# A fused convolution block's output stage: leaky step moved into ScalarE's activation, residual add shared out anew

## The reference

```
x = x + L0(_gn(x), ...)      # two gelu layers
x = x + L1(_gn(x), kernel)   # 4x4 filter
x = x + L2(_gn(x), ...)      # window attention without softmax
x = x + L3(_gn(x), ...)      # 3x3 involution, batch norm, leaky ReLU
```

```
mean = jnp.mean(yout, axis=(0, 1, 2))
var = jnp.var(yout, axis=(0, 1, 2))
yn = (yout - mean) * jax.lax.rsqrt(var + BN_EPS) * gamma + beta
return jnp.where(yn >= 0, yn, LEAKY_ALPHA * yn)
```

## Time and profile before

| | |
|---|---|
| median of 3 runs | 1075.73 us |
| lowest and highest | 1072.3 and 1078.36 us |
| the profiled execution's own time | 1075.53 us |
| its span in the profile | 1072.9 us |
| busy TensorE (matmul) | 783.7 us, 73% of the span |
| busy VectorE | 701.1 us, 65% |
| busy ScalarE | 560.3 us, 52% |
| busy GpSimd | 325.0 us, 30% |

### The profile page before, as it was taken

The page is one execution under the profiler, slowest core; times in us unless marked ns, Lnnn a source line. Parts: engine busy times, 40 slices in busy tenths (PEclk is TensorE's granted clock), DMA queues, the critical chain, the costliest instruction groups (busy, mean ns, idle before and its releaser), DMA issues. The chain is left out here.

```text
span 1072.9 us, 28694 instructions
## 1 busy us (share of the span) xinstructions
PE 783.7 (73%) x12508; PEld 564.6 (53%) x12508; DVE 701.1 (65%) x1085; ACT 560.3 (52%) x581; POOL 325.0 (30%) x265
## 2 busy tenths in 40 slices
PE   5589986897998547844888759979975487346664
PEld 4344442897887437511334319969854384024443
DVE  6556665997555993592223359965459925979993
ACT  4899992342444206357899913424442072525553
POOL 1111111740003880060000026200048700636665
PEclk8899997898999767855799969989986587557776
DMA  9322220000000000000000000000000000003556
GB/s 300 113 64 68 61 71 2 1 2 2 4 4 4 1 1 20 2 0 1 2 2 2 2 1 1 2 2 4 4 4 1 1 20 1 0 1 118 156 157 196
DMA packets 59932, 37.54 MB, mean 35 GB/s; under 512 B 1952, under 2 KB 59424, under 8 KB 59808
## 3 DMA queue, kind: packets, MB, share of 16 engines
q1 hardware_dynamic: 59808, 35.71, 11.0%
HBM read 18.93 MB, written 16.78 MB: 33 GB/s over the span
## 5 line engine op out<-in xcount | busy, mean ns | idle before, releaser
L376 PE MATMUL ps<-work,w2d 32*32 32x512 f32 x2048 | 155.1, 649 | 22.5 <-ACT work L636 15.7
L624 ACT ACTIVATE work<-X,l0s 128x2048 f32<-128x2048 f32 x64 | 133.5, 2089 | 5.1 <-SPq L320 3.8
L363 PE MATMUL ps<-work,cst 32*32 32x512 f32 x2048 | 100.8, 654 | 40.5 <-ACT work L636 21.6
L636 ACT ACTIVATE work<-ps 128x2048 f32<-128x2048 f32 x64 | 119.9, 1873 | 19.3 <-PE ps L363 19.3
L773 DVE SCALAR_TENSOR_TENSOR X<-ps,X 128x1024 f32<-128x1024 f32 x32 | 39.2, 1225 | 136.0 <-PE ps L376 136.0
L1099 POOL TENSOR_TENSOR work<-cst,work 128x512 f32<-128x512 f32 x64 | 69.6, 1109 | 178.7 <-SPq L320 158.0
L376 PEld LDWEIGHTS ps<-work,w2d 32*32 32x32 f32 x2048 | 63.1, 110 | 88.5 <-issue 75.4
L653 ACT ACTIVATE work<-ps 128x512 f32<-128x512 f32 x80 | 47.8, 597 | 110.6 <-PE ps L430 110.6
L441 PE MATMUL ps<-cst,work 128*128 128x143 f32 x640 | 95.2, 294 | 0.2 <-DVE X L823 0.2
L870 DVE TENSOR_TENSOR work<-ps,cst 128x512 f32<-128x512 f32 x64 | 44.3, 692 | 70.7 <-PE ps L477 70.7
L276 PE MATMUL ps<-ST,work 32*128 32x512 f32 x256 | 58.6, 1007 | 43.6 <-DVE work L1005 18.7
(11 more groups left out here) (105 smaller groups left out, 1557.2 us busy)
## 6 DMA issues: line engine op xcount, KB each, us to landing
out<-work SPq DMA_DIRECT2D x64, 256.0 KB, 3.2
work<-x SPq DMA_DIRECT2D x16, 512.0 KB, 5.2
work<-x SPq DMA_DIRECT2D x32, 256.0 KB, 2.9
work<-choose SPq DMA_DIRECT2D x8, 128.0 KB, 2.7
cst<-consts SPq DMA_DIRECT2D x1, 1009.5 KB, 9.5
cst<-consts SPq DMA_DIRECT2D x1, 64.0 KB, 1.9
```

Of the source, the lines that this page charges most:

```text
L363: last = pe.matmul(ps[C * k4:C * k4 + C, g, :], wg[rows, m, C * g:C * g + C], yb[rows, m % 2, k4 * BANK:(k4 + 1) * BANK], start=True, stop ...
L376: last = pe.matmul(ps[C * g:C * g + C, 4 + b, :], diag[rows, m, :], zb[rows, k % ZDEEP, g, :], start=(m == 0), stop=(m == MULTI - 1))
L624: act.activation(yb[:, k % 2, :], X[:, s * PIX + i * CHUNK:s * PIX + (i + 1) * CHUNK], ACT.Gelu, scale=l0s[:, at:at + 1], bias=l0s[:, at + ...
L636: act.activation(zb[:, (s * UNITS + k) % ZDEEP, :, :], ps[:, 0:4, :], ACT.Gelu).then_inc(s_zs, 1)
```

## The change

The activation that applies the batch normalisation's scale and bias uses Prelu with alpha 0.3 instead of Identity, and does the leaky step with it; `leaky` on VectorE is gone. GpSimd now waits for the activation (`s_fy`) instead of for VectorE, and adds the residual to blocks 0 and 1 in one instruction of 128x1024 and to block 2 in one of 128x512. VectorE adds it to block 3 in one scalar_tensor_tensor of 128x512 (`add_last`, (y x 1.0) + x), in the place in its order where `leaky` stood, and raises a semaphore of its own, `s_fd`, for which TensorE waits before it transposes block 3.

```diff
--- before.py
+++ after.py
@@ -119,9 +119,9 @@
 
             return X5[:, ds(s * 4, 4), ds(w, 1), :].rearrange("p b o h -> p (b o) h")
 
-        def group_columns(s, j, b):
-
-            return X[:, s * PIX:(s + 1) * PIX].rearrange("p (b n) -> p b n", b=4)[:, b:b + 2, TILES * j * H:TILES * (j + 1) * H]
+        def group_columns(s, j, b, n):
+
+            return X[:, s * PIX:(s + 1) * PIX].rearrange("p (b n) -> p b n", b=4)[:, b:b + n, TILES * j * H:TILES * (j + 1) * H]
 
         def rows4(v):
             return v.rearrange("p (b h) -> p b h", b=4)
@@ -245,8 +245,8 @@
         s_fc = sem("out_s_spread")
         s_fv = sem("out_v_ready")
         s_fy = sem("out_y_ready")
-        s_fl = sem("out_l_ready")
-        s_fo = sem("out_half_sum_ready")
+        s_fd = sem("out_last_block_sum_ready")
+        s_fo = sem("out_block_sums_ready")
         s_ft = sem("out_transposed")
         s_fe = sem("out_half_laid")
         s_out = [sem(f"group_stored{u}") for u in range(OUT_RING)]
@@ -587,6 +587,8 @@
                         pe.wait_ge(s_fo, 2 * q + b // 2 + 1)
                         if q:
                             pe.wait_ge(s_fe, 2 * q - 1 + b // 2)
+                    if b == 3:
+                        pe.wait_ge(s_fd, q + 1)
                     for n in range(TILES):
                         last = pe.transpose(ps[:, TILES + b, n * P:n * P + P],
                                             row[:, q % OUT_ROWS, b, n * H:n * H + H], ident)
@@ -718,7 +720,7 @@
                 act.wait_ge(s_fv, TILES * q + TILES)
                 s = q // GROUPS
                 y = row[:, q % OUT_ROWS, :, :].rearrange("p b n -> p (b n)")
-                act.activation(y, y, ACT.Identity, scale=bns[:, 12 + s:13 + s], bias=bns[:, 15:16]
+                act.activation(y, y, ACT.Prelu, scale=bns[:, 12 + s:13 + s], bias=bns[:, 15:16], alpha=LEAKY
                                ).then_inc(s_fy, 1)
 
             def lay(q):
@@ -1006,16 +1008,18 @@
                                              vall[:, 4 * s + 3:4 * s + 4], rows4(ps[:, r, :]), ALU.add, ALU.mult
                                              ).then_inc(s_fv, 1)
 
-            def leaky(q):
+            def add_last(q):
+                s, j = divmod(q, GROUPS)
                 dve.wait_ge(s_fy, q + 1)
-                y = row[:, q % OUT_ROWS, :, :].rearrange("p b n -> p (b n)")
-                dve.scalar_tensor_tensor(y, y, LEAKY, y, ALU.mult, ALU.max).then_inc(s_fl, 1)
+                y = row[:, q % OUT_ROWS, 3, :]
+                x_in = X[:, s * PIX + (3 * (W // 4) + TILES * j) * H:s * PIX + (3 * (W // 4) + TILES * (j + 1)) * H]
+                dve.scalar_tensor_tensor(y, y, 1.0, x_in, ALU.mult, ALU.add).then_inc(s_fd, 1)
 
             for q in range(NS * GROUPS):
                 scaled(q)
                 if q:
-                    leaky(q - 1)
-            leaky(NS * GROUPS - 1)
+                    add_last(q - 1)
+            add_last(NS * GROUPS - 1)
 
 
         @block.gpsimd
@@ -1127,10 +1131,10 @@
             pool.tensor_tensor(bns[:, 10:11], bns[:, 10:11], c("root"), ALU.pow).then_inc(s_g, 1)
             for q in range(NS * GROUPS):
                 s, j = divmod(q, GROUPS)
-                pool.wait_ge(s_fl, q + 1)
-                for b in range(0, 4, 2):
-                    y = row[:, q % OUT_ROWS, b:b + 2, :]
-                    pool.tensor_tensor(y, group_columns(s, j, b), y, ALU.add).then_inc(s_fo, 1)
+                pool.wait_ge(s_fy, q + 1)
+                for b, n in ((0, 2), (2, 1)):
+                    y = row[:, q % OUT_ROWS, b:b + n, :]
+                    pool.tensor_tensor(y, group_columns(s, j, b, n), y, ALU.add).then_inc(s_fo, 1)
 
 
 # ---- launch: numpy lays the data out ----
```

## The result

The changed kernel took 1044.87 us (median of 4 executions, 1043.97 to 1053.74) against 1076.53 for the one before in the same comparison: a ratio of 0.973 with a 95% interval of 0.967 to 0.979, 32 us less. The forecast was 1043, in the range 1036 to 1059. The changed kernel's profiled execution lasted 1043.97 us and its span is 1041.5, so 2.5 us lie around it.

The account below looks back on a forecast made before the run. VectorE was taken to be full at 6.9 us a group in the output stage. Last scaling's end at 1019.6 plus a 20.7 us end gave a 1040.3 us span; with 2.63 outside it, forecast 1043 us, range 1036 to 1059.

Parts of the forecast that it names:

- VectorE's bound and its end: Output stage: VectorE is full at 6.9 us a group; without the leaky step its 3.4 us no longer fill it.
- Cycle (c): Output stage: TensorE's transposes wait for ScalarE's copies behind norm; at full clock 9.1 us for two groups, 4.55 each.
- rival 3: Output stage: the cycles overlap better and ScalarE's 4.0 us set the group time; 1037 us, chance 0.03.
- Cycle (b): Output stage: VectorE's add waits behind GpSimd's adds through their lock; two groups in 9.1 us, 4.55 each.
- rival 1: Output stage: TensorE's clock falls back in half the groups, 5.86 us against 4.55; time 1050.5, chance 0.28.
- rival 2: Output stage: TensorE stays at half clock throughout, 5.86 us a group; time 1058.5, chance 0.09.
- The opening: First groups of the output stage: stays as before, 4.94 us a group at half clock, until full clock is granted.
- The end: After the last scaling: the store queue sets it, 4.0 + 14.6 + 2.07 = 20.7 us against 23.6 before.
- Rivals 4 to 6: Half-rate Prelu (0.02); table loads every group, still faster (0.02) or slower (0.03); gain taken back by something unnamed (0.02).
- Rival 4: Output stage: Prelu runs at half the rate, ScalarE needs 6.0 us a group; time 1060, chance 0.02.

Follow-up runs that it names:

- copies first: Changed kernel with the two copies of group q-3 ahead of norm q on ScalarE instead of behind it; 1039.96 us, ratio 0.965.
- fillers: Changed kernel (1045.84 us) and its version with GpSimd adding all blocks (1046.09), each with unread identity transposes added on TensorE.
- half the stores: Changed kernel storing only two of the four images of each group; 1052.4 us, one execution.
- the sharing: Against the kernel before: Identity and VectorE's leaky step kept, VectorE adds block 3, GpSimd three blocks; 1070.5 us, ratio 0.994.
- Prelu alone: Changed kernel with GpSimd adding all four blocks and no add on VectorE; 1049.52 us, ratio to before 0.972.
- again: Changed kernel run once more without edits, giving its second profile; 1046.67 us, ratio 0.970, seven executions from 1041.02 to 1060.93.
- two blocks each: Changed kernel with the residual add shared two blocks on GpSimd and two on VectorE; 1046.05 us, ratio 0.972.

## Why the prediction was right

**VectorE's bound and its end.** The step that carries most of the sum held: without the leaky step VectorE is idle 6.4 us behind the opening, where it had been full, and the groups take 69.0 us from the first scaling's end to the last's, 69.7 by the sum. Prelu at Identity's 2.09 us was right, GpSimd's pair takes 3.6 us where nothing is in between, and VectorE's add 0.69 us when alone.

**Cycle (c), TensorE behind ScalarE's copies.** Right: 9.1 us for two groups by the sum, 9.03 measured. Shown by copies first, which undoes just this wait and took the group to 4.01; the 4.0 of ScalarE's own work, which rival 3 prices, is then reached.

**Cycle (b), the lock, at the same 9.1.** This step was wrong, and it was luck that it cost nothing: (c) stands at the same place. I let VectorE's add wait until GpSimd is through with both its adds. The timeline of the changed kernel shows it waiting for the one in progress: at 984.56 it takes 0.84 us between GpSimd's two adds, and the pair then takes 4.04 us in place of 3.59; at 980.20, just after GpSimd has begun its second, it takes 1.77. With copies first the same work under the same lock went through at 4.01. The Trainium skill, "SBUF — State Buffer", section "Who interferes with whom", has the lock held for a whole instruction, and the trace agrees; between two queued instructions of GpSimd the waiting VectorE gets its turn, which these rows show.

**The clock, rival 1.** The forecast chose full clock throughout and gave 0.28 to falls, with 1050.5. The first profile was the forecast's case. In the second one the clock fell once in every pair of groups from the seventh interval on, and the stage took 97.3 us, 7.6 more, as rival 1 had it (98.0 against 90.4). The pairs were near rival 1's, 10.5 to 10.6 us against 10.4, but not their halves: 6.4 to 6.7 and 3.98 where it had 5.86 and 4.55. The reason for the choice, TensorE's busy share, does not separate the two cases: it was 67% in the first profile's full clock and 8.63 of 13.5 us, 64%, in the second one's before the first fall. So that the median is the forecast's case was in part luck. Of the eleven executions the three longest (1053.74, 1056.76, 1060.93) had a mean granted clock of 0.824, 0.825 and 0.817, the other eight 0.830 to 0.834, which suggests that three of them are of this kind; only two are profiled, and this mean takes in the first 950 us as well. The half clock throughout (rival 2) was not seen.

**The opening.** Right as it was: 4.94, 4.93, 4.94 us, then 4.66 where full clock was forecast with 4.8. That the half clock is what it costs was assumed there and is shown by the fillers (3.98).

**The end and the total.** 20.7 us by the sum and 20.7 measured; half the stores brought it to 16.2. The stage was 0.7 us under the sum (89.7 against 90.4), while the first part ended 1.9 us later than before (951.8 against 949.9), which is inside its scatter; so the 1.9 us between 1044.87 and 1043 say nothing of the mechanism.

**Rivals 4 to 6.** No activation over 2.1 us, no third table load, and the gain was there. (Rival 4's sum is slightly off, 4.18 + 1.92 is 6.1 and gives 1061, and rival 1 starts from 969.8 where the forecast has 969.5; the forecast uses neither.) The Trainium skill, "ScalarE: Activation LUTs", section "Table sets: the hidden batching unit", has the cheap functions in every set; the two loads agree for Copy after Prelu, and show that Prelu itself needed none after Gelu.

**What the parts are worth.** By themselves, the sharing took 7.8 us from the stage and Prelu 24.5 with a falling clock (98.5) or up to 35 with fillers (88.1, of which the faster opening is some 3). Together 33.3 at full clock. Like is to be compared with like: with a falling clock the changed kernel's stage was 97.3 against Prelu alone's 98.5, and with fillers 87.9 against 88.1. So reading the sharing as a part of the gain would be a mistake: in this order of ScalarE's list it fits into time that is lost anyway.

## What to carry to other kernels

When a full engine is relieved, write down the cycle of handovers through the others before adding up work: here no engine had more than 4.0 us of work and the group took 4.5, because a copy that had long been possible stood behind the newest activation in a list. Moving one line took 8.7 us from the stage, 5.1 in the groups and 3.6 in the end, where the whole change had taken 33.3, and only then did the shared add matter. Measure from a mark inside the program, such as the end of a stage's first instruction, where the part ahead of it scatters by more than the effect.

## What was not expected of the hardware

- The same program had its output stage in 89.7 us and in 97.3 us. What set them apart was TensorE's granted clock: in the second, 1.2 GHz came for 3.5 us at a time after stretches in which TensorE was busy 3.81 of 6.75 us.
- Uneven groups, 4.03 to 4.05 and 4.94 to 5.00 us, came just before the first fall in three profiles (again, Prelu alone, two blocks each), and half the stores kept 4.07 and 4.96 through nine intervals before its clock fell, while the changed kernel's first profile had 4.36 and 4.66 and no fall. The lock's wait does not even them out, since the changed kernel kept 4.98 and 4.04 under the same lock; the two forms of the changed kernel differed from the first transposes on, by whether the clock rose during them (3.03 us) or at their end (3.66).
- Twelve transposes of an unused tile behind each of three spreads took the opening's groups from 4.94 to 3.98 us: work that nobody reads paid for itself where it stood in a gap, and 40 of them ahead of a matmul that others waited for made VectorE wait 5.7 us longer for it.
